# A state-space recurrence scanned two units at a time over pairs of PSUM banks

## The reference, cut to what matters

```python
dt = softplus(dt_in @ dt_proj_w.T + dt_proj_b)            # [token, 1024 channels]
dA = exp(dt[..., None] * A)                               # A = -exp(A_log), [1024, 16]
dBx = dtx[..., :, None] * Bg[..., None, :]                # dtx = dt * x
def step(h, inp):                                         # scan over the 512 tokens
    dA_i, dBx_i, C_i = inp
    h = dA_i * h + dBx_i                                  # 1024 x 16 states
    y = einsum('bgn,bgcn->bgc', C_i, h)
    return h, y
y = ys + D_skip * x;  y = y * silu(z);  y @ out_proj_w.T
```

## Time and profile before

| | |
|---|---|
| median of 3 runs | 2874.28 us (2871.49 to 2877.53) |
| the profiled execution's own time | 2876.27 us |
| its span in the trace | 2874.5 us |
| mean granted TensorE clock | 0.944 of full speed |
| PE busy | 2651.7 us, 92% of the span |
| DVE busy | 2129.6 us, 74% |
| ACT busy | 1152.1 us, 40% |
| POOL busy | 1255.9 us, 44% |

### The profile page before, as it was taken

One profiled execution on the slowest core, in us unless ns is written; L12 is line 12 of the kernel. 1 busy time (PEld: TensorE's weight loads), 2 busy tenths in 40 slices (PEclk: granted clock), 3 DMA queues, 4 the chain that ended last, 5 costly groups with the idle time before them and its releaser, 6 DMA issues.

```text
span 2874.5 us, 32445 instructions
## 1 busy us (share of the span) xinstructions
PE 2651.7 (92%) x11096; PEld 1880.8 (65%) x11096; DVE 2129.6 (74%) x2731; ACT 1152.1 (40%) x1690; POOL 1255.9 (44%) x836
## 2 busy tenths in 40 slices
PE   7888888888899878999999999999989999999999
PEld 3443444444344326788887777887877788888887
DVE  4999999999999985543366677777767865555563
ACT  4555555555555534432244443443333322222221
POOL 2789888888889871110010023222212522222220
PEclk8998998989889769999999999999999999999999
DMA  6654654554465436221111112112111111111111
GB/s 230 209 157 121 188 157 121 157 166 129 132 183 154 133 99 231 81 76 49 52 66 59 45 37 67 44 45 67 44 37 45 44 49 48 51 45 52 50 47 66
DMA packets 152310, 275.35 MB, mean 96 GB/s; under 512 B 27345, under 2 KB 27857, under 8 KB 151633
## 3 DMA queue, kind: packets, MB, share of 16 engines
q1 hardware_dynamic: 152144, 273.27, 31.5%
HBM read 178.01 MB, written 61.34 MB: 83 GB/s over the span
## 4 chain that ended last, share of the span: by engine, by line
PE 71%; DVE 11%; ACT 9%; issue 5%; POOL 2%; DMA 1%; SPq 1%; DVEq 0%; POOLq 0%; ACTq 0%
PE ps L1733 19%; PE ps L1734 18%; PE ps L1735 18%; PE ps L1772 8%; DVE state L1358 6%; ACT ps L847 5%; PE ps L1784 4%; POOL read L1172 1%; DMA uraw<-y_d 1%; PE ps L1924 1%; PE ps L1868 1%; PE ps L1898 1%; DVE drive L1349 1%; DVE act_o L1677 0%; POOL xhr L1217 0%
## 5 line engine op out<-in xcount | busy, mean ns | idle before, releaser
L1172 POOL TENSOR_TENSOR read<-state,c_t 128x512 f32<-128x512 f32 x512 | 664.0, 1308 | 138.2 <-DVE state L1358 118.5
L1358 DVE TENSOR_TENSOR_SCAN state<-ps,drive 128x512 f32<-128x512 f32 x512 | 622.3, 1216 | 14.3 <-ACT ps L847 12.8
L1733 PE MATMUL ps<-xh,ghi 128*128 128x512 f32 x1536 | 609.1, 397 | 5.7 <-issue 5.7
L1231 POOL TENSOR_TENSOR wdeq<-packed,scales 128x1024 f32<-128x1024 f16 x96 | 260.2, 2711 | 798.3 <-DVE packed L1510 798.3
L1735 PE MATMUL ps<-xh,glo 128*128 128x512 f32 x1536 | 599.3, 390 | 0.0
L1734 PE MATMUL ps<-xl,ghi 128*128 128x512 f32 x1536 | 599.2, 390 | 0.0
L847 ACT ACTIVATE ps<-ps,a_exp 128x512 f32<-128x512 f32 x512 | 338.9, 662 | 473.8 <-PE ps L1772 472.5
L1772 PE MATMUL ps<-dpack,sel 128*128 128x512 f32 x512 | 260.9, 510 | 114.2 <-DVE state L1358 112.1
L1677 DVE TENSOR_TENSOR act_o<-act_o,ps 128x512 f32<-128x512 f32 x192 | 131.7, 686 | 313.4 <-PE ps L1735 298.5
L1349 DVE TENSOR_TENSOR drive<-ps,b_t 128x512 f32<-128x512 f32 x512 | 344.1, 672 | 12.7 <-PE ps L1772 11.9
L1099 ACT ACTIVATE ahi<-act_o 128x512 fp32r<-128x512 f32 x192 | 121.4, 632 | 562.6 <-DVE act_o L1677 562.6
(11 more groups left out here) (204 smaller groups left out, 3775.3 us busy)
## 6 DMA issues: line engine op xcount, KB each, us to landing
whi<-w_d SPq DMA_DIRECT2D x63, 256.0 KB, 4.1
wlo<-w_d SPq DMA_DIRECT2D x63, 256.0 KB, 4.6
dpack<-dh SPq DMA_DIRECT2D x64, 128.0 KB, 3.8
dpack<-dl SPq DMA_DIRECT2D x64, 128.0 KB, 3.6
b_d<-ev SPq DMA_DIRECT2D x32, 256.0 KB
x_d<-ev SPq DMA_DIRECT2D x32, 256.0 KB, 2.6
vpack<-vh SPq DMA_DIRECT2D x64, 128.0 KB, 3.5
vpack<-vl SPq DMA_DIRECT2D x64, 128.0 KB, 2.8
```

What stands on the lines that cost most here:

```text
L1172: pool.tensor_tensor(read[:, n % RRING, :], state[:, n % SRING, :], c_t[:, g % 2, :], ALU.mult).then_inc(read_ready, 1)
L1231: pool.tensor_tensor(wdeq[:, :].rearrange("p (h n) -> p h n", h=2), codes, scale, ALU.mult).then_inc(deq, 1)
L1358: dve.tensor_tensor_scan(state[:, n % SRING, :], ps[:, n % 2, :], drive[:, n % DRING, :], 0.0, ALU.mult, ALU.add)\
L1733: pe.matmul(out_, w_h, x_h, start=(start and k == 0), stop=False)
```

## The change

Two units make a **pair** `m` (`PAIRS` = 8 in a step). What it does:

- `make_drive(m)`, `scan(m)` and `read_out(g, k)` each work on 128 x 1024 elements. The scan runs through two banks as one row of 1024. The first element of the decay of every odd unit must then be zero, so that the state begins anew: column 0 of `dh` and `dl` is zeroed once and left alone, and the exponential of odd units leaves column 0 out.
- The decays have four banks in turn (0 to 3), the drives' inputs the two banks 4 and 5 as one pair, the gathered sum bank 6, and projections and dt share bank 7. Six lead jobs still use banks 5 and 6.
- PE issues spreads in fours, once per two units: `spread_v` of the next pair (waiting for the drive of this pair), then `spread_dt` of the next pair (waiting for the scan of the pair before this).
- The slices of a job stand as 2, 1, 1, 0 (`JOB_SLOTS`) behind its four units. `take` is one unit later. `dt_project` stands behind unit 12 instead of 10, and `soft_abs` and `soft_pos` both behind unit 12.
- `soft_one` goes to SBUF (`sp_log`) instead of PSUM, `soft_rest` reads it there and stands in the next step ahead of that step's first scan; `soft_log` follows behind unit 1 and waits for it. Some softplus buffers now share memory and have waits for that.
- `w_low` and `split_lo` of the recurrence move from DVE to POOL, and two `normalise` groups move from steps 2 and 4 to steps 5 and 7.

The core of the diff:

```diff
+PAIRS = NST // 2
+LEAD_JOBS = 6
+JOB_SLOTS = ((0, 1), (2,), (3,), ())
@@ memory
-    drive = place("drive", [P, DRING, S], F32, after())
+    drive = place("drive", [P, DRING, 2, S], F32, after())
@@ ACT
 def soft_abs(q):
     act.wait_ge(dtp_ready, q + 1)
     if q:
         act.wait_ge(sp_exp_ready, q)
+        act.wait_ge(sp_sum_ready, q)
 def soft_log(q):
-    if q:
-        act.wait_ge(dt_ready, q)
+    act.wait_ge(sp_rest_ready, q + 1)
 def decay(g, c):
-    act.activation(ps[:, n % 2, :], ps[:, n % 2, :], ACT.Exp,
+    bank = ps[:, n % 4, n % 2:S]
+    act.activation(bank, bank, ACT.Exp,
                    scale=a_exp[:, col:col + 1]).then_inc(decay_ready, 1)
@@ ACT, in the loop over units
-if jobs and c % 4 == 2 and c > 4:
-    take(first + c // 4 - 1)
+if jobs and c % 4 == 3 and c < 12:
+    take(first + c // 4)
 if 0 <= g + 1 < STEPS:
+    if c == 1 and g:
+        soft_log(g + 1)
...
     if c == 12:
         soft_abs(g + 2)
-    if c == 13:
         soft_pos(g + 2)
     if c == 14:
         soft_exp(g + 2)
     if c == 15:
         soft_one(g + 2)
-        soft_log(g + 2)
@@ POOL
+at, src = n % RRING, n % SRING
+pool.tensor_tensor(read[:, at:at + 2, :], state[:, src:src + 2, :],
+                   over_tiles(c_t[:, g % 2, :], 2), ALU.mult).then_inc(read_ready, 1)
@@ POOL, in the loop over pairs
+if g in (CT - 5, 2 * CT - 5, 3 * CT - 5) and k % 2 == 1:
+    split_lo(g // CT + 1, k // 2)
+if jobs and k % 2 == 1 and k < 6 and first + k // 2 + 2 < IN_TILES:
+    w_low(first + k // 2 + 2)
@@ DVE
+def make_drive(m):
+    dve.wait_ge(vb_ready, 2 * m + 2)
+    dve.tensor_tensor(drive[:, m % DRING, :, :], ps[:, 4:6, :], over_tiles(b_t[:, g % 2, :], 2),
+                      ALU.mult).then_inc(drive_ready, 1)
+def scan(m):
+    dve.wait_ge(drive_ready, m + 1)
+    dve.wait_ge(decay_ready, 2 * m + 2)
+    at, bank = 2 * m % SRING, 2 * (m % 2)
+    dve.tensor_tensor_scan(flat(state[:, at:at + 2, :]), flat(ps[:, bank:bank + 2, :]),
+                           flat(drive[:, m % DRING, :, :]), 0.0, ALU.mult, ALU.add)
@@ DVE, the loop
+for j in range(PAIRS):
+    m = PAIRS * g + j
+    if m + 1 < PAIRS * STEPS:
+        make_drive(m + 1)
+    if j == 0 and 1 <= g < STEPS - 1:
+        soft_rest(g + 1)
+    scan(m)
...
+    if g >= 1 and j == 3:
+        skip_y(g - 1)
@@ PE
 def spread_v(n):
     if n >= 2:
-        pe.wait_ge(drive_ready, n - 1)
-    spread(vpack[g % 2], 2 + n % 2, c, vb_ready)
+        pe.wait_ge(drive_ready, n // 2)
+    spread(vpack[g % 2], 4 + n % 2, c, vb_ready)
 def spread_dt(n):
-    if n >= 2:
-        pe.wait_ge(scan_done, n - 1)
-    spread(dpack[g % 2], n % 2, c, dtb_ready)
+    if n >= 4:
+        pe.wait_ge(scan_done, n // 2 - 1)
+    spread(dpack[g % 2], n % 4, c, dtb_ready)
@@ PE, in the loop over units
-        if n + 1 < NST * STEPS:
-            spread_v(n + 1)
-        spread_dt(n)
+        if c % 2 == 0 and n + 2 < NST * STEPS:
+            spread_v(n + 2)
+            spread_v(n + 3)
+            spread_dt(n + 2)
+            spread_dt(n + 3)
         if jobs and c < 12:
-            project(first + c // 4, c % 4)
-        if nb < B and c == 10:
+            for f in JOB_SLOTS[c % 4]:
+                project(first + c // 4, f)
+        if nb < B and c == 12:
             dt_project(g + 2)
```

More of the change, by code:

```diff
@@ L109, in build @@
     gather = place("gather", [P, NST // 4, P // 4], F32, after())
[L110 to L116 removed]
+    SP = after()
+    sp_abs = place("sp_abs", [P, S], F32, SP)
+    sp_rest = place("sp_rest", [P, S], F32, SP)
+    sp_pos = place("sp_pos", [P, S], F32, SP + 2048)
+    dt_t = place("dt_t", [P, S], F32, SP + 2048)
+    sp_log = place("sp_log", [P, S], F32, SP + 4096)
+    v_t = place("v_t", [P, S], F32, SP + 4096)
+    sp_exp = place("sp_exp", [P, S], F32, SP + 6144)
+    SP_END = SP + 12288
+    row_r = place("row_r", [P, S], F32, SP_END)
     row_u = place("row_u", [P, S], F32, after())
@@ L221, in build @@
         consts_ready = sem("consts_ready")
-        x_loaded = [sem(f"x_loaded{b}") for b in range(B)]
+        x_loaded = [None] + [sem(f"x_loaded{b}") for b in range(1, B)]
+        zeroed = sem("zeroed")
         mean_loaded = sem("mean_loaded")
@@ L1409, in _ @@
             dve.tensor_copy(ident16[:, :], ident[:, :]).then_inc(consts_ready, 1)
[L1410 removed]
+            make_drive(0)
             for g in range(STEPS):
                 nb, k, jobs = step_jobs(g)
[L1413 to L1425 removed]
+                for j in range(PAIRS):
[5 more added lines that the diff above has]
+                    scan(m)
+                    for b in (1, 2, 3):
+                        if g == CT * b - 6 and j % 2 == 0:
+                            scale_x(b, j // 2)
+                    if g >= 1 and j == 3:
                         skip_y(g - 1)
[L1427 to L1429 removed]
+                    if nb and jobs and k == 0 and j == 1:
                         dt_split(nb)
[L1431 to L1432 removed]
             skip_y(STEPS - 1)
@@ L1827, in _ @@
             pe.wait_ge(ln_centred, FT * B)
-            pe.wait_ge(ln_u, 3)
+            pe.wait_ge(ln_u, B)
             spread_v(0)
+            pe.wait_ge(job_taken, taken_count(4))
+            spread_v(1)
+            spread_dt(0)
+            spread_dt(1)
             for g in range(STEPS):
```

158 lines of the change are left out of this document (70 added, 88 removed).

## The result

| | before | after |
|---|---|---|
| median | 2874.35 us (4 runs, 2871.49 to 2877.53) | 3040.76 us (4 runs, 3039.59 to 3046.94) |
| span of the profiled execution | 2874.5 us | 3045.2 us |
| recurrence, first scan's start to last scan's end | 78.0 to 1062.1: 984 us | 80.2 to 1228.5: 1148 us |
| mean granted clock | 0.944 | 0.914 |

The changed kernel takes 1.0583 times as long (95% interval 1.0565 to 1.0601). Of the 171 us between the spans 164 lie in the recurrence, 2 ahead of it and 4 behind.

The account below looks back on a forecast made before the run. DVE was taken to bound the recurrence; 26 job steps of 34.95 us (909), four of 30.6 (122), two last steps (55) and small terms made 1105 against 984, +121, so 2995 us for the median; range 2900 to 3070.

Parts of the forecast that it names:

- rival 1: Clock falls twice or more in each job step, one further heavy pair running low: 62 us more, 3057; chance 0.16.
- What pairing saves: DVE's drives and scans: a pair takes 3.32 us against 3.44, saving 0.12 x 256 = 31 us.
- PE's burst at pair 0: First job of a step: slices and gather delay spread_v at low clock; DVE waits 2.5 us, with soft_rest in the gap.
- The burst at pair 2: Second job of a step: nine matmuls and a gather ahead of spread_v make DVE wait 0.95 us.
- The burst at pair 4: Third job of a step: skip_y takes 0.65 of the gap, so DVE waits only 0.3 us.
- The softplus: ACT between decays 12 and 13: scan 6 waits 2.2 us at full clock, 3.3 at low, in each of 30 steps.
- The clock's allowance: Longer low-clock falls of PE meeting one of three waits: 1.0 us more per job step.
- Jobless steps: Steps 5, 13, 21, 29: 28.0 + 2.2 + 0.4 = 30.6 us each, times 4 = 122.
- Low words on POOL: w_low and split_lo moved off DVE: 24 us gained there, hidden on POOL, 3 us given for late dt_x.
- Rival 2: Bursts of slices hidden by earlier spreads, only the softplus wait left: 28 us more than now, 2902; chance 0.11.
- rival 3: Faster: larger fixed cost per instruction saved and both added waits absorbed, 81 us less, 2793; chance 0.07.
- rival 4: POOL becomes the bound, a read pair over 3.5 us: job step 35 or more, 3000 and up; chance 0.04.

Follow-up runs that it names:

- experiment 3: Changed kernel with soft_one in PSUM again and a short soft_rest ahead of scan 7 of the step before: 3062.41 us.
- experiment 6: Changed kernel with softplus behind unit 13, one slice per unit, and short soft_rest (soft_one in PSUM) ahead of scan 7: 2926.21 us.
- experiment 9: Kernel before, each spread_v behind a unit without a slice issued two more times on PE: 2853.08 us.
- experiment 11: Changed kernel, softplus behind unit 13, one slice per unit, short soft_rest, spread_v ahead of the odd slice, dt_low and v_low one read earlier on POOL: 2909.89 us.
- experiment 10: As experiment 11, and with repeats of spread_v behind units without slices: 2879.12 us.
- experiment 8: Kernel before with only w_low and split_lo of the recurrence moved from DVE to POOL: 2869.70 us.
- experiment 2: Changed kernel with one slice of a job behind each unit instead of 2, 1, 1, 0: 2964.82 us.

## Why the prediction came out as it did

The forecast was slower, 2995 us, with a range to 3070; it is slower, 3041. The mechanism was the one named; 46 us are a matter of sizes. By its number alone, 3041 lies nearer to rival 1 (3057). And part of the agreement is luck: the waits of a job step were put at 6.95 in all and are 7.0, but drive 2 got 1.1 less than forecast and the other three places 1.15 more. Of the signs that were named, job steps of 34 to 36 us and jobless ones near 30 did not come (35 to 38, and 33 to 35), nor did the order of the waits (2 to 4 at pair 2, near 1 at pair 4: 1.42 and 1.62).

- **What pairing saves.** Right: 1.12 and 2.20 between starts, 3.32 a pair as worked out. The 0.96 per ns in the working does not follow from the two widths that it names (0.58 and 1.175 give 0.86); drive to drive, 0.58 and 1.12, and scan to scan, 1.14 and 2.20, do give 0.95 and half of 0.97. The rule of the Trainium skill (VectorE: DVE Perf Modes, TRN2 errata) would have had 80 us; the gaps between starts show 31 again, and the length of one scan (2.28 for twice the 1.21) agrees with it only in that the fixed part isn't doubled.
- **PE's burst at pair 0.** `soft_rest` and wait were put at 0.7 + 2.5 = 3.2 and are 1.9 + 1.42 = 3.3: the sum is right, its parts are not. `soft_rest` takes 1.97, not 0.7; by experiments 3 and 6 that costs next to nothing in a job step, as the burst releases drive 2 no earlier. The clock is low at this place in all 26 job steps (0.59 to 0.85 in the 4.2 us ahead of drive 2), as forecast.
- **The burst at pair 2** was put at 0.95 and is 1.62 on average: 1.21 to 1.27 in 14 of the 26 job steps, at clock 1.00, and 2.15 to 2.83 in seven, at 0.70 to 0.77 (again over the 4.2 us ahead of the drive). The rows shown give the 0.3 that are missing at the full clock: the first slice starts 0.63 after scan 1's end, not 0.52; the gather begins 0.32 after the matmul ahead of it, not 0.23; and the first matmul of the slice behind it needs 0.34 to the next, not 0.23.
- **The burst at pair 4** was put at 0.3, with 1.0 for the clock in all, and is 1.42, of the four waits the one that was missed by most. At clock 1.00 it is 0.58 to 0.61 in seven job steps, late by the same 0.3 as pair 2's. In 15, where the clock is 0.69 to 0.81, it is 2.11 to 2.17, as in the timeline shown. The rows of the granted clock there:

```profile
680.00:681.00 1.00, 0.76 (x3) 0.62 (x4) 1.00 (x3) 0.37 (x2) 0.73 (x1) 0.82 0.00 0
...
683.00:684.00 1.00, 1.00 (x6) 0.20 (x8) 1.00 (x1) 0.00 (x0) 0.88 (x1) 0.50 0.94 328
684.00:685.00 1.00, 1.00 (x9) 0.19 (x2) 0.16 (x1) 0.00 (x0) 0.00 (x0) 0.98 0.77 287
```

- **The softplus** was put at 2.2 (3.3 at the low clock) and is 2.55 on average: right. It is 2.29 to 2.33 in the 16 steps where the clock is 1.00 while ACT waits for the projection, and 3.38 in four where it is 0.50. 30 times, as said.
- **The clock's allowance** was too small, and so were the bursts. Rival 1, that the clock falls twice or more in a step, is what happened: beside the fall at drive 2 there is one at drive 4 or drive 6 in 23 of the 26 job steps, and in ten a third ahead of scan 6. But a fall at those drives adds some 1.5, not the 3.4 of the rival, since it doesn't last the whole burst. With the two bursts and the softplus, 4.45 was forecast, clock included, and 5.6 measured: 1.15 a step, 30 us over 26 steps. At the full clock the three are 1.25, 0.59 and 2.3, 4.1 where 3.45 was worked out. So some 0.7 of the 1.15 was mis-sized at the full clock, and some 0.45 is the clock beyond its 1.0. The rule of the Trainium skill (TensorE: Matmul & The Clock Gate, HAM oscillation) that bursts between waits begin throttled fits the run of 680 to 684, where PE had waited in turn for scans and drives; other bursts of the same step began at the full clock. What the clock costs in the whole program, experiments 9 and 11 against 10 price: 22 and 31 us.
- **Jobless steps** were put at 30.6 and are 33.3 to 34.9, some 14 us over four. Here nothing hides `soft_rest`'s 1.97, the clock is at 0.70 to 0.79 in the two stretches shown, and scan 6 waits up to 3.4. These and the 30 above come near the 43 us by which the recurrence was missed (1148 for 1105). They are not all of it: the last stretch shown took 30.0 where 27.3 was forecast for a step without softplus.
- **Low words on POOL** were put at 24 gained and 3 lost. In the kernel before they gain 6 (experiment 8), since POOL is full in the early steps. In the changed kernel this could not show, with DVE waiting there anyway; it was not run by itself.
- Rival 2 (bursts hidden) fell by experiment 2, rival 3 (faster) by the waits, and rival 4 by POOL's 25.2 busy in 37.

What stays open: how much of the first five steps' wait for `vpack` is POOL's and how much the transfers'; the paired kernel with all cures and the low words on DVE again, which was not run; and 6 us of the span that lie ahead of and behind the recurrence.

## What to carry to other kernels

Halving the number of instructions of the full engine pays the gap between starts, read in the timeline, here 0.12 us a pair, and not the difference of lengths. It also doubles the unit of hand-over: with the same banks the other engines get their orders in bursts, half as often, and whatever stands between two spreads counts twice; work out for each hand-over what is queued ahead of it, at both clock levels. Before shortening an instruction, ask whether its engine would wait in that place anyway; and where PE is thin but must answer quickly, try repeated matmuls in its idle stretches. Here they took 22 us off the kernel before, while the pairs, with every cure that was tried, came no lower than 2879 us.
